# A stacked attention operand kept as three distinct slots, with the other three copied inside SBUF

## The reference, cut to what matters

```python
h = einsum('bhid,oi,od->bho', x, weighted_sum, weight)          # first stage
q, k, v = heads(norm(h) @ Wq + bq), heads(norm(h) @ Wk + bk), heads(norm(h) @ Wv + bv)
c2p = take_along_axis(einsum('bhqd,hpd->bhqp', q, pos_k), idx)  # 16 heads, 512 x 512
p2c = take_along_axis(einsum('bhkd,hpd->bhkp', k, pos_q), -idx)
scores = (einsum('bhqd,bhkd->bhqk', q, k) + c2p + p2c.T) / sqrt(48)
h = h + (softmax(scores) @ v) @ Wo + bo
h = h + experts(norm(h))
```

## Time and profile before

| | |
|---|---|
| median of three runs | 5230.35 us |
| the profiled execution | 5219.19 us |
| its span, first to last instruction | 5217.3 us |
| TensorE (PE) busy | 4616.0 us, 88% |
| VectorE (DVE) busy | 3521.8 us, 68% |
| ScalarE (ACT) busy | 2588.1 us, 50% |
| GpSimd (POOL) busy | 1926.1 us, 37% |
| DMA | 1461.31 MB, mean 280 GB/s; HBM read 738.61 MB, written 715.94 MB |

### The profile page before, as it was taken

One profiled execution on the slowest core, in us unless ns is written; L12 is line 12 of the kernel. 1 busy time (PEld: TensorE's weight loads), 2 busy tenths in 40 slices (PEclk: granted clock), 3 DMA queues, 4 the chain that ended last, 5 costly groups with the idle time before them and its releaser, 6 DMA issues. The chain is left out here.

```text
span 5217.3 us, 110895 instructions
## 1 busy us (share of the span) xinstructions
PE 4616.0 (88%) x31272; PEld 3287.5 (63%) x31272; DVE 3521.8 (68%) x9058; ACT 2588.1 (50%) x4809; POOL 1926.1 (37%) x4461
## 2 busy tenths in 40 slices
PE   6999999499999999999999999999999996771698
PEld 4666666266666666666666666666666664661565
DVE  2333333388888888878888878878888885775511
ACT  1222222266666666666666666666666661110021
POOL 1222222144444444444444444444444443550022
PEclk9999999799999999999999999999999997885599
DMA  4767767699999999999999999999999995771033
GB/s 133 231 225 235 226 221 237 207 346 350 349 344 343 350 337 347 348 332 343 347 334 351 345 335 346 350 332 344 349 341 348 343 342 170 253 237 61 9 94 68
DMA packets 672172, 1461.31 MB, mean 280 GB/s; under 512 B 48195, under 2 KB 290291, under 8 KB 671603
## 3 DMA queue, kind: packets, MB, share of 16 engines
q1 hardware_dynamic: 665462, 1446.22, 81.7%
q0 software_dynamic: 6144, 8.52, 1.0%
HBM read 738.61 MB, written 715.94 MB: 279 GB/s over the span
## 5 line engine op out<-in xcount | busy, mean ns | idle before, releaser
L1010 DVE CUSTOM_DVE_ANT_1 a_scored<-a_ps_m_s,a_bias 128x512 f32<-128x512 f32 x2048 | 1398.8, 683 | 573.6 <-PE a_ps_m_s L878 542.3
L947 ACT ACTIVATE a_probsT<-a_ps_m_t 128x512 f32<-128x512 f32 x2048 | 1227.0, 605 | 923.5 <-PE a_ps_m_t L887 922.1
L887 PE MATMUL a_ps_m_t<-a_ident,a_scored 128*128 128x128 f32 x8192 | 1260.2, 277 | 0.5 <-ACT a_probsT L947 0.5
L941 ACT ACTIVATE a_skew_in<-a_ps_m_tab 128x512 f32<-128x512 f32 x2048 | 1125.8, 614 | 205.3 <-POOL a_high L808 92.8
L887 PEld LDWEIGHTS a_ps_m_t<-a_ident,a_scored 128*128 128x128 f32 x8192 | 934.0, 141 | 437.8 <-DVE a_scored L1017 359.4
L1017 DVE TENSOR_SCALAR a_scored<-a_scored,a_top_of 128x512 f32<-128x512 f32 x2048 | 1042.7, 529 | 0.0
L818 POOL COPY a_bias<-a_high 128x128 f32<-128x128 f32 (+1 forms) x1024 | 355.6, 376 | 1786.1 <-DMA a_bias<-d_skew 1779.7
L827 POOL TENSOR_SCALAR_AFFINE_SELECT a_bias<-a_bias 128x128 f32<-128x128 f32 (+2 forms) x2560 | 979.8, 409 | 71.9 <-POOL a_bias L827 63.1
L878 PE MATMUL a_ps_m_s<-a_ident,a_bias 128*128 128x128 f32 x5120 | 900.6, 273 | 0.0
L859 PE MATMUL a_ps_m_tab<-a_tabs,a_stack 96*128 96x256 bf16 (+1 forms) x4096 | 714.0, 276 | 196.0 <-ACT a_skew_in L941 123.2
L878 PEld LDWEIGHTS a_ps_m_s<-a_ident,a_bias 128*128 128x128 f32 x5120 | 682.1, 142 | 109.0 <-issue 2.3
(11 more groups left out here) (182 smaller groups left out, 3649.2 us busy)
## 6 DMA issues: line engine op xcount, KB each, us to landing
d_skew<-a_skew_in SPq DMA_DIRECT2D x1024, 480.0 KB, 7.5
a_bias<-d_skew SPq DMA_DIRECT2D x512, 896.0 KB, 8.9
a_stack<-d_stack SPq DMA_DIRECT2D x256, 384.0 KB
p_xt<-in_xT SPq DMA_DIRECT2D x32, 2048.0 KB, 9.3
d_ctx<-a_ctx_sb SPq DMA_DIRECT2D x128, 256.0 KB, 7.7
d_stack<-p_part_q SPq DMA_DIRECT2D x64, 384.0 KB, 2.8
d_stack<-p_part_k SPq DMA_DIRECT2D x64, 384.0 KB, 3.4
d_v<-p_v_sb SPq DMA_DIRECT2D x32, 544.0 KB, 3.0
```

What stands on the lines that cost most here:

```text
L887: mm = pe.transpose(m_t[:, k % 2, t * P:(t + 1) * P], scored[:, hh % SCORED, t, k * P:(k + 1) * P], ident[:])
L941: nc.scalar.activation(skew_in[:, u, w, 2 * half:2 * half + 2], m_tab[:, w], ACT.Identity).then_inc(tab_kept, 1)
L947: nc.scalar.activation(turned_at(hh // GH, hh % GH, k), m_t[:, k % 2], ACT.Exp, scale=SCALE).then_inc(turned, 1)
L1010: nc.vector.tensor_tensor_reduce(split(scored[:, hh % SCORED, t]), split(m_s[:, t % 2]), extra, 1.0, -3.0e38, ALU.add, ALU.max, top_of[:, ...
```

## The change

Only three slots of the stack are written to DRAM and loaded; the parts of k lie in reverse order, so that slots 0 to 2 hold the pairs (0, 2), (1, 1), (2, 0). In SBUF they lie interleaved in rows 0 to 47. Slots 3 to 5 repeat parts that are there already, and six DMAs within SBUF copy them (16 partitions, taken from every third row, into 16 neighbouring ones: rows 48 to 63, 64 to 79, 80 to 95; 64 KB each, in pieces of 1 KB). A load now serves four heads, in four buffers, and the copies of a load are issued four heads after it, ahead of the table store of that head. TensorE waits for key terms and copies instead of for the load.

```diff
--- before.py
+++ after.py
@@ -48,10 +48,12 @@
 PITCH = 2 * ROW
 AHEAD = 4
 SLOTS = 6
-SIDE_A = (0, 0, 0, 1, 1, 2)
-SIDE_B = (0, 1, 2, 0, 1, 0)
-RUNS = ((0, 3), (3, 5), (5, 6))
+PARTED = 3
+SIDE_A = (0, 1, 2, 0, 0, 1)
+SIDE_B = (2, 1, 0, 0, 1, 0)
+COPIES = ((0, 3, 0), (0, 4, 0), (0, 5, 1), (1, 3, 2), (1, 4, 1), (1, 5, 2))
 ST = SLOTS * HD
+SB = PARTED * HD
 PLAIN = 3
 TERMS = 6
 ROWS = ST + TERMS + PLAIN
@@ -61,8 +63,8 @@
 LEAD = 5
 NEXT = 3
 SCORED = 4
-SH = 2
-SR = 8
+SH = 4
+SR = 4
 GH = 4
 NG = NH // GH
 NS = NH // SH
@@ -113,7 +115,7 @@
 
         passed = sem("passed")
         d_tab = dram("d_tab", (2, 3, H, TW), BF16)
-        d_stack = dram("d_stack", (B, NH, HD, SLOTS, SW), BF16)
+        d_stack = dram("d_stack", (B, NH, HD, PARTED, SW), BF16)
         d_plain = dram("d_plain", (PLAIN, NH, TW), BF16)
         d_kterm = dram("d_kterm", (B, TERMS, NH, S), BF16)
         d_v = dram("d_v", (B, S, NH * VROW))
@@ -355,7 +357,7 @@
     h_out = [sem(f"p_h_out{u}") for u in range(2)]
     v_out, t_out = sem("p_v_out"), sem("p_t_out")
     parts_out = [sem(f"p_parts_out{u}") for u in range(2)]
-    DMAS = 2 * len(RUNS) * HC
+    DMAS = 2 * HC
     CH = 2 * HC
     pairs = B // 2
 
@@ -377,10 +379,8 @@
                     settled(sp, parts_done, (CH + 1) * (n + 1), passed)
                     for c in range(HC):
                         to = d_stack[n, c * NH // HC:(c + 1) * NH // HC].rearrange("h d j x -> (h d) j x")
-                        for j0, j1 in RUNS:
-                            of = part_q[:, u, SIDE_A[j0], c].unsqueeze(1).to_broadcast([P, j1 - j0, S])
-                            sp.dma_start(to[:, j0:j1, 0:S], of).then_inc(parts_out[u], 16)
-                            sp.dma_start(to[:, j0:j1, S:], part_k[:, u, 0:j1 - j0, c]).then_inc(parts_out[u], 16)
+                        sp.dma_start(to[:, :, 0:S], part_q[:, u, :, c]).then_inc(parts_out[u], 16)
+                        sp.dma_start(to[:, :, S:], part_k[:, u, :, c]).then_inc(parts_out[u], 16)
                     to = d_kterm[n].rearrange("t h x -> h t x")
                     sp.dma_start(to[:, 0:3], part_t[0:NH]).then_inc(t_out, 16)
                     sp.dma_start(to[:, 3:], part_t[NH:]).then_inc(t_out, 16)
@@ -495,7 +495,7 @@
                     ins = nc.scalar.activation(part_q[:, u, 0, c], src, ACT.Identity,
                                                bias=qk_bias[:, 0, c:c + 1])
                 else:
-                    for out in (full_k[:, c], part_k[:, u, 0, c]):
+                    for out in (full_k[:, c], part_k[:, u, 2, c]):
                         ins = nc.scalar.activation(out, src, ACT.Identity, bias=qk_bias[:, 2, c:c + 1])
                 ins.then_inc(qk_kept, 1)
 
@@ -542,7 +542,7 @@
 
                 after(pool, parts_done, (CH + 1) * (n - 1) + m + 1 if not isinstance(n, int) or n else 0)
                 left, full, part = ((rest_q[:, c], full_q[:, c], part_q[:, u, 0, c]) if m < HC else
-                                    (rest_k[:, c], full_k[:, c], part_k[:, u, 0, c]))
+                                    (rest_k[:, c], full_k[:, c], part_k[:, u, 2, c]))
                 nc.gpsimd.tensor_tensor(left, full, part, ALU.subtract).then_inc(low_done, 1)
 
             def batch(n, u, more):
@@ -603,7 +603,7 @@
                 if m < HC:
                     a, mid, low = rest_q[:, c], part_q[:, u, 1, c], part_q[:, u, 2, c]
                 elif m < CH:
-                    a, mid, low = rest_k[:, c], part_k[:, u, 1, c], part_k[:, u, 2, c]
+                    a, mid, low = rest_k[:, c], part_k[:, u, 1, c], part_k[:, u, 0, c]
                 else:
                     a, mid, low = full_t[:], part_t[:, 1], part_t[:, 2]
                 nc.vector.tensor_copy(mid, a).then_inc(mid_done, 1)
@@ -670,6 +670,7 @@
     const_in, past_in, zeroed, zeroed_p, past_kept = (
         sem("a_" + n) for n in ("const_in", "past_in", "zeroed", "zeroed_p", "past_kept"))
     stack_in = [sem(f"a_stack_in{u}") for u in range(SR)]
+    slots_in = [sem(f"a_slots_in{u}") for u in range(SR)]
     values_in = [sem(f"a_values_in{u}") for u in range(2)]
     skew_out = [sem(f"a_skew_out{u}") for u in range(2)]
     bias_in = [sem(f"a_bias_in{u}") for u in range(AHEAD)]
@@ -677,7 +678,8 @@
      pv_done, ctx_kept, ctx_out) = (sem("a_" + n) for n in (
          "tab_done", "tab_kept", "high_kept", "parted", "filled", "s_done", "s_kept", "lowered",
          "turn_done", "turned", "pv_done", "ctx_kept", "ctx_out"))
-    STACKS = 2
+    SLOT_DMAS = 1 + len(COPIES)
+    assert NS == SR
     HEADS = B * NH
     PARTS = 6
     TURN = 2
@@ -710,17 +712,26 @@
             for w in range(2):
                 for j in range(SLOTS):
                     part = (SIDE_B if w == 0 else SIDE_A)[j]
-                    sp.dma_start(tabs[j:ST:SLOTS, w],
-                                 d_tab[w, part].rearrange("(h d) x -> d h x", d=HD)).then_inc(const_in, 16)
+                    rows = tabs[j:SB:PARTED, w] if j < PARTED else tabs[j * HD:(j + 1) * HD, w]
+                    sp.dma_start(rows, d_tab[w, part].rearrange("(h d) x -> d h x", d=HD)).then_inc(const_in, 16)
             sp.wait_ge(zeroed_p, 2)
             sp.dma_start(tabs[ST + TERMS:, 1], d_plain).then_inc(const_in, 16)
 
             def load_stack(b, g):
                 u = g % SR
-                sp.dma_start(stack[0:ST, u], d_stack[b, g * SH:(g + 1) * SH].rearrange("h d j x -> (d j) h x")
+                sp.dma_start(stack[0:SB, u], d_stack[b, g * SH:(g + 1) * SH].rearrange("h d j x -> (d j) h x")
                              ).then_inc(stack_in[u], 16)
                 sp.dma_start(stack[ST:ST + TERMS, u, :, S:], d_kterm[b, :, g * SH:(g + 1) * SH]
-                             ).then_inc(stack_in[u], 16)
+                             ).then_inc(slots_in[u], 16)
+
+            def copy_slots(b, g):
+
+                u = g % SR
+                settled(sp, stack_in[u], 16 * (b + 1), passed)
+                for side, to, of in COPIES:
+                    at = slice(side * S, (side + 1) * S)
+                    sp.dma_start(stack[to * HD:(to + 1) * HD, u, :, at], stack[of:SB:PARTED, u, :, at]
+                                 ).then_inc(slots_in[u], 16)
 
             def load_values(b, half):
                 sp.dma_start(values[:, half],
@@ -757,6 +768,8 @@
             sp.wait_ge(zeroed_p, 4)
             for g in range(SR - 1):
                 load_stack(0, g)
+            for g in range(SR - 2):
+                copy_slots(0, g)
             load_values(0, 0)
             load_values(0, 1)
             for m in range(LEAD):
@@ -775,6 +788,8 @@
                         if not (last and g >= NS):
                             settled(sp, s_done, QT * n, passed)
                             load_stack(b + g // NS, g % NS)
+                        if not (last and g > NS):
+                            copy_slots(b + (g - 1) // NS, (g - 1) % NS)
                     if not (last and hh + LEAD >= NH):
                         write_tables(n + LEAD, (hh + LEAD) % NH, hh + LEAD)
 
@@ -851,7 +866,7 @@
 
                 g, w, half = hh // SH, part % 2, part // 2
                 if hh % SH == 0 and part == 0:
-                    after(pe, stack_in[g % SR], 16 * STACKS * (NS // SR * b + g // SR + 1))
+                    after(pe, slots_in[g % SR], 16 * SLOT_DMAS * (b + 1))
                 after(pe, tab_kept, 4 * n + part - 1)
                 for k in range(2):
                     at = (S if w else 0) + (2 * half + k) * P
```

## The result

The changed kernel took 5517.53 us (median of 4 runs, 5508.5 to 5529.9) against 5230.08 us before (4 runs, 5222.91 to 5236.2): a ratio of 1.0551, 95% interval 1.0535 to 1.0568. The profiled execution took 5508.5 us, its span 5506.6. Slower was forecast, but by 80 us and not 287: the time lies above the range. HBM read fell to 688.28 MB and written to 665.61 MB, 50 MB less each way, as the change says.

What follows compares the result with a forecast made beforehand. TensorE bounds the first stage; TensorE and a full DMA stream together bound attention. From 5219.19 us, +65 (stream), +26 (SP's queue), -5 and -3 (seams) give 5302, stated as 5310; own range 5255 to 5400, 8 in 10 5130 to 5500.

Steps and rivals of the forecast that it cites:

- the two seams: End of the first stage, fewer stores, -5 us; start of the attention, smaller loads with twelve copies, -3 us.
- the term of SP's queue: Issue order on SP in the attention stage: delayed table stores against fewer load collisions, +26 us, ends -77 and +154.
- the bursts: Load, key terms and copies ahead of a table store at every fourth head: up to 154 us, a third taken.
- the loads' new place: Stack load no longer collides with values and ctx in two heads a batch: up to 77 us back, a third taken.
- 2.05 us a group: Engine time of six copies within SBUF per four heads, taken at 192 GB/s; ends 1.05 and 3.36 us.
- its own bound: Attention stage: a lighter DMA stream could give back at most what DMA costs TensorE today, 136 us over 512 heads.
- The stream's rates: DMA speed by partitions touched: 208 GB/s of engine time for 48-partition loads, 192 for copies; net +65 us.
- Rival 2: Attention stage: full price of narrow transfers, copies at 117 GB/s and load at 183, 5514 us; chance 0.20.
- Rival 1: Attention stage: HBM relief, 50 MB less each way and copies at 373 GB/s, 5142 us; chance 0.27.

Runs made afterwards that it cites:

- g4_only: Kernel before with four heads a load (768 KB), same bytes, no copies: 5454.03 us, ratio 1.0426.
- third buffer: `skew_in` with three buffers in place of two: 5187.51 us on the kernel before, 5426.39 us on the changed kernel.
- tiny_aside: Changed kernel with its six copies replaced by six 4 KB DMAs (64 B pieces) to a side buffer, scores incomplete: 5467.41 us.
- wide_aside: Changed kernel with its copies replaced by six of the same size over 64 partitions of a side buffer, scores incomplete: 5525.56 us.
- rows_spread: Changed kernel with each copy's target taken as every third row of 48 to 95, not 16 neighbouring rows: 5525.80 us.
- copies_late: Changed kernel with the six copies issued behind that head's table store, not ahead of it: 5406.38 us.
- before_3skews: Kernel before with three `skew_in` buffers in place of two: 5187.51 us, ratio 0.9944.

## Why the prediction was wrong

**The mechanism.** Right: the direction, the stage, the full stream, ScalarE and TensorE behind it, the 50 MB, and that the waits for load and copies are met. Of the two seams one was right. The end of the first stage moved from 981.24 to 976.07, 5.2 us (forecast 5; its last stores also began 0.8 us earlier). But the first table read moved only from 1023.40 to 1021.15, and that is both seams together: 2.3 us where 8 were forecast. From the end of the stage to that read it took 45.1 us for 42.2, so the start of the attention lost 2.9 us where 3 were to be gained; its twelve copies held SP for 7.68 us.

**The step that failed is the term of SP's queue, and in it the regrouping of the loads:** "Against that the stack load leaves the two heads a batch where it collides with values and ctx today: up to 2.4 us, 77 us back", and then "I take a third of both: +26 us". That is +51 for the bursts and -26 for the loads' new place. Loading four heads at a time, alone, costs 224 us (`g4_only`). Beside it the other terms held better:

| step, two buffers | entered in the sum | measured |
|---|---|---|
| four heads a load | -26 | +224 |
| half the bytes (stream 1.54 us a group, seams) | -197 - 8 | -176 |
| six copies (2.05 us a group, bursts) | +262 + 51 | +239 |

The regrouping is off by 250 us; the other two are off by 29 and by -74. What was missed: one load of 768 KB holds up the landing of the table store behind it (11.1 us for 8.7), the copies hold up its issue (10.4 us after the last for 6.4), and `skew_in` with two buffers has no slack for either.

**The order of the steps matters**, so the table is no law. With the third buffer the first two steps together are worth nothing either way (5195 beside 5188), and the copies cost 231. The prediction should have stopped at its own bound: it said that at most 136 us could come back in this stage and netted 197 us of relief against the copies. `g4_only` had more waits to give back (82.8 us per 1000 before the tables, for 32.5), and there 176 us did come back. What the smaller loads give without the regrouping was not run.

**The stream's rates** were near what was measured. The bare loads ran at 201 GB/s and share 1.01 (I had used 208 of engine time). The stretch with the twelve copies shows 162 at 0.94, so 172 (I had used 192), but the end of the three loads is in it too, and no run times the copies' own rate. What failed is the stream as the price of everything: "at a share of 1.00 the stream's extra time passes on almost one for one" was read from a share that `tiny_aside` shows at 0.98 with 37 GB/s less than before. And "four more DMAs a group cost their completions only: nothing" does not hold: six DMAs with hardly a byte cost 182 to 189 us.

**An issue of a copy** took 0.65 us inside the stream (3.89 / 6) and 0.64 with nothing computing (7.68 / 12), just over my 0.3 to 0.6; the burst delays the store by 3.9 us, its load and key terms by 3.0 more. The cost of six issues without bytes is above the upper end of 154 that I gave the whole term. And the stall came two heads later, not three.

**The clock was left out.** The event in the earlier trace rows cost 1.19 us; TensorE was busy 3.72 of the 5 us around it and stayed at full clock:

```profile
2480.00:2485.00 5.00, 3.72 (x32) 3.02 (x30) 3.10 (x10) 3.61 (x8) 1.91 (x7) 1.00 1.04 350
2485.00:2490.00 5.00, 4.90 (x41) 3.19 (x39) 3.98 (x11) 3.51 (x8) 2.80 (x8) 1.00 1.03 381
```

The longer stalls of the changed kernel take the clock with them: 85 us of the run (its whole rise in busy time), 100 by the 0.20 us a head. So the price read from this short stall was too low for the longer ones.

**The rivals.** Rival 2 named 5514, 4 us from the result, and for a wrong reason: its narrowness is excluded by `wide_aside` and `rows_spread`. That it came so close is luck: it priced the copies at nearly twice what they cost (3.36 us a group, 430 us) and took the regrouping as relief, like the forecast. The range for 8 in 10 also ended at 5500, under this rival's own number. Rival 1 is excluded: even with no copies at all the kernel is 39 us slower than before, and the changed one shows a share of 1.00, where this rival wanted under 0.97. The relief it counted on exists (176 us) but is less than what the regrouping costs.

**What stays open.** How issue time and bytes share the 231 us that the copies cost with the third buffer. Each explains three quarters alone. Two things both may do are a later table store and a later read; reads with a longer lead were not tried. What remains of the regrouping's cost with a third buffer is open too.

## What to carry to other kernels

Price a regrouping of transfers as a change of its own, also when it moves the same bytes: fewer, larger loads cost 4.3% here. Look at what stands behind them, in the issuing queue and in landing, and at how many buffers cover its delay. In a stream that is full beside an engine that is nearly full, don't net a removal one for one against an addition: over today's kernel the removal can give back at most what the other engine waits today. Count a small DMA by its issue, and where the trace shows a lower clock after long stalls, price that with them.

## What the runs showed of the hardware

- A DMA of 4 KB and one of 64 KB cost SP about the same to issue. In `tiny_aside` (its timeline): three took 1.87 us, 0.62 each.

```profile
2499.64 1.87 SPq L736 DMA_DIRECT2D a_aside<-a_aside  x3
```

- ScalarE took 1.16 us for each of the same 64 KB copies (6.96 / 6) where SP took 0.65.
- A table store behind a stack load landed after 8.7 us when the load had 384 KB (`before`) and after 11.1 us when it had 768 KB (`g4_only`), medians at 2000 to 3000 us.
- Copies within SBUF into 16 partitions, into 64, and into every third row gave the same time of the kernel.
- The DMA busy share stays at 0.97 to 1.01 between 306 and 346 GB/s (0.98 at 306 in `tiny_aside`, 0.97 at 324 in `copies_late`, 1.00 at 346 in `before_3skews`), so in this range it does not tell how much the engines move.
